# One set of 256 columns for all value products, the moved split and router product, and the batch loop written out

## What is computed

```python
q, k, v = split_heads(Wq x + bq), split_heads(Wk c + bk), split_heads(Wv c + bv)
q, k = rotary(q), rotary(k)
scores = einsum('bhtc,bhsc->bhts', q, k) / sqrt(8)          # 256 x 256 for each of 64 x 8 heads
out = einsum('bhts,bhsc->bhtc', softmax(scores), v)
x = x + Wo out + bo
w = top 2 of softmax(norm(x) Wr + bias), normalised           # the router, 16 experts
x = x + sum over the 2 of w * (silu(n Wg) * (n Wu)) Wd  +  shared expert
```

## Time and profile before

| | |
|---|---|
| median of 3 executions | 879.17 us (878.0 to 880.91) |
| the profiled execution | 880.23 us, of which the span from the first to the last instruction is 878.4 us |
| busy in the span | PE 743.0 us (85%), DVE 627.2 us (71%), ACT 512.1 us (58%), POOL 450.4 us (51%) |
| mean granted TensorE clock | 0.945 of full speed |
| program rows listed in order | PE 732, DVE 594, ACT 368, POOL 326, SP 215 (the loop's turn listed once) |

### The profile page before, as it was taken

How to read it: one execution, slowest core, us unless ns; L and a number is a source line. 1 busy time by engine, 2 the same in 40 slices (tenths; PEclk the granted TensorE clock), 3 DMA queues, 4 the chain that set the end, 5 groups by cost and what they waited for, 6 DMA issues and landing times. The chain is left out here.

```text
span 878.4 us, 23052 instructions
## 1 busy us (share of the span) xinstructions
PE 743.0 (85%) x6138; PEld 530.9 (60%) x6139; DVE 627.2 (71%) x1653; ACT 512.1 (58%) x1213; POOL 450.4 (51%) x929
## 2 busy tenths in 40 slices
PE   3699999999999999999999999962899299999900
PEld 2356666766766666666666666531566188888700
DVE  6877898898899888888888899638333134444467
ACT  3155777777777777777777777651555045555400
POOL 5444555645645555555564563122777535656510
PEclk9999999999999999999999999985799799999965
DMA  8597344444444444444434469720222345555379
GB/s 255 137 301 220 107 125 122 105 128 124 109 120 113 125 114 118 123 106 129 121 105 127 123 177 287 237 68 1 97 106 106 124 117 153 145 155 156 98 227 347
DMA packets 112404, 126.46 MB, mean 144 GB/s; under 512 B 14189, under 2 KB 98928, under 8 KB 112369
## 3 DMA queue, kind: packets, MB, share of 16 engines
q1 hardware_dynamic: 105456, 109.11, 45.0%
q0 software_dynamic: 6912, 16.93, 5.2%
HBM read 76.93 MB, written 50.63 MB: 145 GB/s over the span
## 5 line engine op out<-in xcount | busy, mean ns | idle before, releaser
L797 DVE TENSOR_REDUCE M<-bank_s 128x2 f32<-128x512 f32 x512 | 339.7, 685 | 60.6 <-PE bank_s L1050 55.3
L600 ACT ACTIVATE Pr<-bank_st 128x512 f32<-128x512 f32 x512 | 295.6, 598 | 122.9 <-PE bank_st L1078 117.8
L1050 PE MATMUL bank_s<-QK 72*128 72x256 bf16 x1024 | 201.4, 280 | 13.1 <-DMA QK<-parts 11.1
L1078 PE MATMUL bank_st<-QK 98*128 98x256 bf16 x1024 | 197.8, 275 | 1.3 <-ACT Pr L600 1.1
L1033 PE MATMUL bank_o<-Pr,wide 128*32 128x256 f32 x2048 | 139.5, 388 | 0.0
L1050 PEld LDWEIGHTS bank_s<-QK 72*128 72x128 bf16 x1024 | 93.3, 102 | 70.7 <-DVE M L797 34.3
L525 POOL TENSOR_TENSOR work<-work 128x256 f32<-128x256 f32 x64 | 46.8, 731 | 162.6 <-DVE work L855 162.6
L940 DVE TENSOR_TENSOR OT<-work,bank_st 128x128 f32<-128x128 f32 x112 | 32.2, 288 | 136.2 <-ACT work L681 136.2
L1078 PEld LDWEIGHTS bank_st<-QK 98*128 98x128 bf16 x1024 | 97.8, 98 | 27.4 <-ACT Pr L600 4.6
L571 POOL DMA_INDIRECT results<-QK,ids_out x80 | 78.4, 980 | 64.9 <-issue 49.4
L1184 PE MATMUL bank_st<-wgu,xT_sb 128*128 x320 | 84.4, 387 | 0.0
(11 more groups left out here) (145 smaller groups left out, 1218.5 us busy)
## 6 DMA issues: line engine op xcount, KB each, us to landing
QK<-parts SPq DMA_DIRECT2D x128, 288.0 KB
parts<-parts_sb SPq DMA_DIRECT2D x128, 96.0 KB, 2.3
slots<-xT_sb SPq DMA_DIRECT2D x8, 1300.0 KB, 6.3
wide<-slots SPq DMA_DIRECT2D x80, 130.0 KB, 2.3
ctx_kv<-ctx_dram SPq DMA_DIRECT2D x64, 128.0 KB, 2.1
QK<-results SPq DMA_DIRECT2D x16, 512.0 KB, 8.2
X<-x_dram SPq DMA_DIRECT2D x8, 512.0 KB, 7.8
parts<-parts_sb SPq DMA_DIRECT2D x64, 64.0 KB, 2.1
```

The lines of the kernel that those rows point to most:

```text
L600: nc.scalar.activation(Pr[k][:], bank_st[k % 2][:], ACT.Exp, scale=SCALE).then_inc(s_exp, 1)
L797: nc.vector.tensor_reduce(M[:, c, 2 * k:2 * k + 2], bank_s[S_BANK[c][k]][:].rearrange("p (a s) -> p a s", a=2), AX.X, ALU.max).then_inc(s_ ...
L1050: last = nc.tensor.matmul(bank_s[S_BANK[at.mod(2)][k]][:, T * t:T * t + T], Q[c][0:KR, k, P * t:P * t + P], K[c][0:KR, k, :], start=True, ...
L1078: last = nc.tensor.matmul(bank_st[k % 2][:, T * s:T * s + T], K[c][0:MROW + 2, k, P * s:P * s + P], Q[c][0:MROW + 2, k, :], start=True, st ...
```

## The change

1. The heads go through the pipeline in the order 0, 2, 4, 6, 1, 3, 5, 7 (`ORDER`). The first group of four is then the even heads, the second the odd ones.
2. Both groups add into the same 256 columns of `bank_o`. Head j of the odd group takes its 32 stationary columns from 9 columns before its own block of `V`, where the end of the block before is zero, so that its 8 channels and its sum come out in rows 9 to 17 of the 32 rows; the even group's are in rows 0 to 8. The first product of the even group starts the sum, the last of the odd group ends it.
3. `O` has 256 columns instead of 512, its copy on ACT is 128x256, and PE transposes two tiles instead of four. The division reads the other layout with the same number of elements.
4. The split of the maxima leaves DVE for POOL, and stands there in the same step as the last maximum, ahead of the last of the five operations for batch r + 6, which waits behind it. Its first operation waits for all eight maxima of the step.
5. The router product stands after ST of k = 2, directly ahead of TM, instead of after ST of k = 1.
6. `LOOP = None`: all 77 steps of the attention are written out on all five engines. `held`, with which PE waits for a bank, then waits for all readers of the bank in each step and not for the main one alone.
7. `fresh` is `Pr[7]` instead of `O`.

```diff
+    ORDER = (0, 2, 4, 6, 1, 3, 5, 7)
...
-        O = sb("O", [P, 2 * T])
+        Vcols = [wide[:, 1024 * i:1024 * i + 1024] for i in range(2)]
+        O = sb("O", [P, T])
...
-        fresh = O
+        fresh = Pr[7]
...
-        LOOP = (8, 56)
+        LOOP = None
...
+                if at.has(2):
+                    c = at.mod(2)
+
+                    wait(pool, s_red, at.value(8, 24))
+                    wait(pool, s_TM, at.value(1, 1))
+                    nc.gpsimd.tensor_tensor(Mb[:, c, 0, :], M[:, c, :], newton[:, 2:3].to_broadcast([P, 2 * H]),
+                                            ALU.subtract).then_inc(s_hi, 1)
+                    wait(pool, s_hi, at.value(1, 3))
+                    nc.gpsimd.tensor_tensor(Mb[:, c, 1, :], M[:, c, :], Mb[:, c, 0, :],
+                                            ALU.subtract).then_inc(s_msp, 1)
+                if at.has(6):
+
+                    p, h = at.odd_pair(6), at.mod(2)
                     wait(pool, s_p2, at.value(1, 7))
                     nc.gpsimd.tensor_tensor(parts[:, p, h, 2, :], rest[:, h], parts[:, p, h, 1, :],
                                             ALU.subtract).then_inc(s_pt, 1)
...
-                        nc.scalar.activation(O[:], bank_o[:], ACT.Copy).then_inc(s_Oe, 1)
+                        nc.scalar.activation(O[:], bank_o[:, 0:T], ACT.Copy).then_inc(s_Oe, 1)
...
-                        nc.vector.tensor_reduce(M[:, c, 2 * k:2 * k + 2],
+                        nc.vector.tensor_reduce(M[:, c, 2 * ORDER[k]:2 * ORDER[k] + 2],
...
-                    if k == 0 and at.has(1):
-                        c = at.mod(2, 1)
-
-                        wait(dve, s_red, at.value(8, 16))
-                        wait(dve, s_TM, at.value(1, 0))
-                        nc.vector.tensor_copy(Mb[:, c, 0, :], M[:, c, :]).then_inc(s_hi, 1)
-                        wait(dve, s_hi, at.value(1, 2))
-                        nc.vector.tensor_tensor(Mb[:, c, 1, :], M[:, c, :], Mb[:, c, 0, :],
-                                                ALU.subtract).then_inc(s_msp, 1)
...
-                        h = 4 * group + j
-                        last = nc.tensor.matmul(bank_o[32 * j:32 * j + 32, T * group:T * group + T],
-                                                V[at.odd_pair(off)][:, chunk, b, h, :],
-                                                Pr[h][:, T * chunk:T * chunk + T],
-                                                start=(chunk == 0), stop=(chunk == 1))
+                        first = 32 * (H * (2 * chunk + b) + 2 * j + group) - (D + 1) * group
+                        last = nc.tensor.matmul(bank_o[32 * j:32 * j + 32, 0:T],
+                                                Vcols[at.odd_pair(off)][:, first:first + 32],
+                                                Pr[4 * group + j][:, T * chunk:T * chunk + T],
+                                                start=(group == 0 and chunk == 0), stop=(group == 1 and chunk == 1))
...
-                            for g in range(2):
-                                col = P * (2 * t + g)
-                                last = nc.tensor.transpose(bank_a[:, col:col + P],
-                                                           O[:, T * g + P * t:T * g + P * t + P], ident[:])
+                            last = nc.tensor.transpose(bank_a[:, P * t:P * t + P], O[:, P * t:P * t + P], ident[:])
```

More of the change, by code:

```diff
@@ L289, in xattn_moe @@
         FIRST, LAST = -8, 69
-        LOOP = (8, 56)
+        LOOP = None
         def steps(eng, step, first=FIRST, loop=LOOP, last=LAST, turn=4):
-            for b in range(first, loop[0]):
+            for b in range(first, loop[0] if loop else last):
                 step(Step(b, None, turn))
+            if not loop:
+                return
             with eng.Fori(loop[0] // turn, loop[1] // turn) as i:
@@ L857, in step @@
                     if k == 5 and at.has(-1):
-                        o = bank_a[:].rearrange("p (g e) -> p g e", e=32)
+                        o = bank_a[:, 0:T].rearrange("p (a j e) -> p a j e", a=2, e=32)[:, :, :, 0:2 * D + 2]
+                        o = o.rearrange("p a j (g e) -> p a j g e", g=2)
                         wait(dve, s_T1, at.value(1, 0))
                         wait(dve, s_On, at.value(1, -1))
-                        nc.vector.reciprocal(rden[:], o[:, :, D]).then_inc(s_rc, 1)
+                        nc.vector.reciprocal(rden[:].rearrange("p (a j g) -> p a j g", a=2, g=2),
+                                             o[:, :, :, :, D]).then_inc(s_rc, 1)
                         wait(dve, s_rc, at.value(1, 0))
@@ L868, in step @@
                         nc.vector.tensor_tensor(
-                            On[at.odd_pair(-1)][:, :, C * half:C * half + C].rearrange("p a (h e) -> p a h e", e=D),
-                            o[:, :, 0:D].rearrange("p (a h) e -> p a h e", a=2),
-                            rden[:].rearrange("p (a h o) -> p a h o", a=2, o=1).to_broadcast([P, 2, H, D]),
+                            On[at.odd_pair(-1)][:, :, C * half:C * half + C]
+                            .rearrange("p a (j g e) -> p a j g e", g=2, e=D), o[:, :, :, :, 0:D],
+                            rden[:].rearrange("p (a j g o) -> p a j g o", a=2, g=2, o=1)
+                            .to_broadcast([P, 2, H // 2, 2, D]),
                             ALU.mult).then_inc(s_On, 1)
@@ L1078, in step @@
                             last = nc.tensor.matmul(bank_st[k % 2][:, T * s:T * s + T],
[L1079 to L1080 removed]
+                                                    K[c][0:MROW + 2, ORDER[k], P * s:P * s + P],
+                                                    Q[c][0:MROW + 2, ORDER[k], :], start=True, stop=True)
                         last.then_inc(s_ST, 1)
@@ L1085, in step @@
                         nc.tensor.matmul(bank_b[:, 0:T], w[:, 5, :], OT[:], start=True, stop=True).then_inc(s_WO, 1)
+                    if even and k == 2 and at.has(-6):
+                        if at.i is None and at.r == 6:
+                            pe.wait_ge(s_wr, 32)
+                        held(at, bank_b, (s_xte, at.pairs(-6, add=1), NP))
+                        for c in range(2):
+                            last = nc.tensor.matmul(bank_b[:, 0:E], xTs[0][:, c, :], wr[:, c, :],
+                                                    start=(c == 0), stop=(c == 1))
+                        last.then_inc(s_lg, 1)
                     if k == 2 and at.has(1):
@@ L1094, in step @@
                         values(at, 1)
[L1095 to L1103, removed]
                     if k == 4 and at.has(-1):
```

2 lines of the change are left out of this document (1 added, 1 removed).

## The result

The changed kernel takes 852.76 us (median of 4 executions, 849.22 to 857.81), the kernel before 880.04 us (878.0 to 883.65): a ratio of 0.969, interval 0.963 to 0.975. The forecast was 853 us. The profiled execution took 857.81 us, the longest of the four and 5 us above the median; its span is 856.0 us.

The account below looks back on a forecast made before the run. PE was taken to bound the even part (98 to 516 us): 0.43 + 0.40 + 0.08 = 0.91 us a pair, 22.8 us over 25 pairs, with 3.5 outside 26.3 us off 879.17, so 853 us; range 843 to 869 us.

Parts of the forecast that it names:

- Bound and pair: Attention's even part, 98 to 516 us: PE rests at only two places, and two steps take 16.79 us.
- Transposes: On PE: four fewer in two steps at a pitch of 0.108 us, gaining 0.43 us a pair.
- Router product: On PE: S and ST of k = 2 fill its wait for `xT_sb`; gain 0.40 us a pair, 0.36 of 0.76 stays.
- Split: On POOL: ready 0.1 us before both TMs; the odd step's 0.16 us stall goes, gaining 0.08 us a pair.
- rival of the stall at TM: POOL 0.3 us later than taken, both TMs stand 0.2 us, pair gains 0.51, 863 us; chance 0.20.
- Written out: Attention without the hardware loop: zero effect on PE, bounds of 0.1 us a pair, 2.5 us in all, either way.
- Value products at an offset: On PE, stationary columns at an offset of 9: taken as zero, at most 0.1 us a step, 5 us in all.
- DVE as cover: DVE loses 29 us of 369.6 in the even part, to about 81% busy; no gain itself, cover for the shorter step.
- Outside the even part: Gains of 1.0 us at 30 to 98 us, 1.0 at 516 to 563 and 1.5 at 563 to 600.

Follow-up runs that it names:

- undo_split: Changed kernel with the split of the maxima back on DVE at k = 0; 851.04 us, ratio 0.967 to the kernel before.
- split_last: Changed kernel with the split on POOL behind the fifth operation of 128x256 instead of ahead of it; 861.88 us.
- undo_router: Changed kernel with the router product after ST of k = 1 again; 864.65 us, ratio 0.981 to the kernel before.
- undo_merge: Changed kernel with natural head order, 512 columns, 128x512 copy and four transposes again; 865.79 us, ratio 0.980 to the kernel before.
- spread_fill: Changed kernel with the eight slot-blanking writes issued at steps 16, 20, ... 44 instead of 56 to 63; 846.49 us, ratio 0.962 to the kernel before.
- values_first: Changed kernel with values and TM ahead of ST of k = 2 in even steps; 848.37 us, ratio 0.966 to the kernel before.
- loop_back: Changed kernel with the hardware loop over steps 8 to 55 again; 850.53 us, ratio 0.965 to the kernel before.
- after_again: The changed kernel unaltered, timed again on another chip; 905.45 us, ratio 0.969 to the kernel before there.
- best: Changed kernel with values_first, spread_fill and expert weights in twelve 512 KB loads; 888.43 us, 0.950 of the kernel before on the same chip as after_again.

## Why the prediction was right, point by point

- *Bound and pair.* PE without rest but for two stalls, 16.79 us a pair: right, and confirmed by a pair of 15.79 us: the two stalls were 0.76 and, on average, 0.08, and 0.25 is left.
- *Transposes*, 0.43: measured 0.43. The price is the pitch. The figure of about 275 ns on the page "TensorE: Matmul & The Clock Gate" of the Trainium skill (Part 4) is again the duration (mean 275 ns in the changed kernel) and not what a transpose costs PE here.
- *Router product*, 0.40 with 0.36 of the stall left: measured 0.43 by undoing it, 0.40 alone. What stayed is 0.25, in two pieces, and the first piece is ST of k = 2 waiting for the exponential, as written. This term was a little small: by my working TM comes 1.55 us behind ST of k = 1 (300.08 to 301.63), and it came after 1.47. These 0.08 us and the 0.03 by which I rounded down are enough for the 0.09 by which the pair got shorter than forecast (1.0 us less, and not 0.91).
- *Split*, 0.08 and margins of 0.1 us: the stall of 0.16 is gone from the odd TM, and undoing the move costs 0.09, but in the even step (undo_split above), so the two numbers agree in part by luck. The margins were too small in the forecast. The split is over 0.31 (305.89 to 306.20) and 0.37 us (298.05 to 298.42) before TM. I had started the split 0.08 us behind the fourth operation; it starts before that operation's row ends (305.38 against 304.75 + 0.67), its second operation starts 0.29 us after the first where I had allowed up to 0.47, and in the odd step the fourth operation came 0.1 us sooner before TM. So the rival of the stall at TM was further off than its chance of 0.20 says, and split_last shows that it was a real one: 0.7 us later costs 0.5 us a pair, not the 0.7 to 0.8 of that run's expectation, which let both TMs stall. By the rule of the "GPSIMD Engine Reference" of the Trainium skill (Engine selection), work with two inputs is about twice as slow there as on VectorE; an estimate by it is 0.36 us for each operation of the split. The trace disagrees: it has 0.21 and 0.22 us against 0.18 on DVE for L807 in the earlier trace rows, where the mean of that line is 312 ns.
- *Written out*, zero: 0.04 a pair, 1 us, inside the bounds.
- *Value products at an offset*, zero: no difference in pitch.
- *DVE as cover.* Right, and its load was not needed: undo_split does not make S wait.
- *Outside the even part*, 3.5 us gained: this term was too large, and how far is open. In the profiled executions it measured -2.8 us, nothing gained in the start and 2.3 lost in the fill stage. By the medians the kernel gained 27.3 us (26.4 against the 879.17 of the forecast), of which 25.2 lie in the even part, and 1 to 2 us are left for the rest. I had shrunk the steps there by a share for the DMA's load and put the clock at nothing. PE waits for `QK` there, 3.7 us at 60 to 100 us and 1.6 at 485 to 565 against 2.6 and 0.8 before, and behind such waits the clock was at its lower level, for longer in some executions than in others. That the shorter steps make these waits longer is argued from one profile of the kernel before, not shown.

So the fit of the total to 0.3 us is in part luck: the even part gave 2.4 us more than forecast, the rest of the kernel about 2 us less.

The start differs from run to run of near kernels: TM of batch 7 begins at 101.0 and 102.0 us in the two profiles of the changed kernel, at 99.8, 99.9, 99.3 and 99.1 us in those of undo_router, undo_merge, spread_fill and values_first, and at 97.0, 96.1 and 98.5 us in undo_split, loop_back and split_last. The stage from TM of batch 57 to 63 goes from 45.7 us (undo_split) to 51.4 in the kernels that keep the transfers where they were. But for the changed kernel I have read this from one profile of each; whether it belongs to the kernel or to the single execution stays open. Together the two stages are large enough for the few us by which undo_split and loop_back come out ahead in spite of their longer pairs.

## What to carry to other kernels

Where PE runs dense, price an instruction of PE by its distance to the next start, and a wait by its distance less that pitch; then such terms add to a few hundredths of a microsecond. A product that waits for a copy is best moved behind work that is ready, and before moving it again one asks who is next to wait (here ST of k = 2). Where transfers load a stage, a shorter compute path gave little or nothing here. There the order of the transfers is worth trying, in pieces small enough not to hold up the loads that the next step needs: weights in pieces of 1.5 MB cost up to 1.7 us a pair, in pieces of 512 KB up to 0.5. And a stage whose clock changes from one execution to the next can't be judged by one profile.

## What the runs showed of the hardware

- In the changed kernel's profile a wait of PE of 2.4 us for `QK`, ending at 80.54 us, was followed by a granted clock of 0.50 from 81 to 87 us, and one of 1.3 us, ending at 525.91, by 0.50 from 528 to 537 us. In after_again, the same kernel in another execution, the second was 0.9 us and had 0.50 from 529 to 532 us only behind it. In best two waits of 0.6 us (509 to 511 us) were followed by 0.50 from 513 to 522 us.
- A transpose of 128x128 shows 275 ns and costs 110. The 16 fp32 records of the value products, 256 columns in four column groups, take 1.01 us to the next S, about 0.25 us for each four.
- A subtraction of 128x16 takes 0.21 to 0.22 us on POOL, with 0.29 from start to start where one waits for the other; 128x1 takes 0.19 and 128x256 0.67.
- Between the first timing and that of the last group the same kernel differed by 50 us behind the attention, and by 3 us at its end (TM of batch 63 at 547.0 and 544.2 us). Its cause stays open.
